# A twelve-layer decoder on one core: where the norms' inverse square roots are computed

## The reference, cut to what matters

```python
x = x + sublayer(_layernorm(x, axis=-1), ...)
# _layernorm: (x - mean) / sqrt(var + 1e-5)
```

## Time and profile before

| | |
|---|---|
| median of 3 runs | 1956.75 us (1954.98 to 1956.88) |
| the profiled execution, its own time | 1954.65 us |
| its span, first to last instruction | 1953.2 us |
| PE, DVE, ACT, POOL busy | 78%, 63%, 42%, 36% of the span |
| mean granted TensorE clock | 0.826 of full speed (2.4 GHz) |

### The profile page before, as it was taken

The page is one execution under the profiler, slowest core; times in us unless marked ns, Lnnn a source line. Parts: engine busy times, 40 slices in busy tenths (PEclk is TensorE's granted clock), DMA queues, the critical chain, the costliest instruction groups (busy, mean ns, idle before and its releaser), DMA issues. The chain is left out here.

```text
span 1953.2 us, 26886 instructions
## 1 busy us (share of the span) xinstructions
PE 1528.4 (78%) x8610; PEld 1058.0 (54%) x8610; DVE 1235.1 (63%) x3228; ACT 818.4 (42%) x2168; POOL 702.9 (36%) x975
## 2 busy tenths in 40 slices
PE   4899987799999589996953981154787689948998
PEld 3566754588888323334742550023555379944665
DVE  4587775365555688983347239896888679953222
ACT  1244431144333478883143113311777368811111
POOL 1488840066655457671001004343555222110000
PEclk8799995899999755556986995576899879958999
DMA  5100002000000155553000011101000300000000
GB/s 200 52 7 7 1 12 92 11 2 7 6 1 1 35 98 96 91 92 114 1 0 0 0 39 51 38 1 54 1 1 2 129 2 2 2 1 1 1 0 22
DMA packets 98379, 62.20 MB, mean 32 GB/s; under 512 B 88896, under 2 KB 93376, under 8 KB 96448
## 3 DMA queue, kind: packets, MB, share of 16 engines
q1 hardware_dynamic: 98240, 60.48, 11.6%
HBM read 38.44 MB, written 1.05 MB: 20 GB/s over the span
## 5 line engine op out<-in xcount | busy, mean ns | idle before, releaser
L101 PE MATMUL banks<-arena_a,normed_t 128*128 128x512 f32 (+3 forms) x736 | 281.9, 533 | 11.7 <-PEq L2963 11.7
L425 POOL TENSOR_TENSOR lut_weights<-lut_weights,arena_b 128x536 f32<-128x536 f32 x128 | 179.2, 1400 | 211.6 <-DVE arena_b L415 201.7
L101 PEld LDWEIGHTS banks<-arena_a,normed_t 128*128 128x128 f32 x736 | 140.6, 211 | 123.0 <-issue 120.0
L584 POOL TENSOR_SCALAR work<-work,small 128x256 f32<-128x256 f32 (+1 forms) x384 | 178.3, 482 | 76.5 <-DVE small L576 76.5
L101 PE MATMUL banks<-arena_a 64*128 64x512 bf16 (+1 forms) x384 | 161.7, 540 | 34.4 <-PEq L2963 18.6
L1506 ACT ACTIVATE arena_a<-banks,work 128x1024 uint8<-128x1024 f32 x128 | 154.1, 1204 | 48.3 <-DVE work L1450 40.5
L1448 DVE TENSOR_REDUCE work<-banks 128x1 f32<-128x1024 f32 x128 | 155.3, 1214 | 22.6 <-PE banks L101 22.6
L1535 POOL TENSOR_SCALAR arena_a<-arena_a 128x1024 bf16<-128x1024 uint8 x128 | 132.8, 1045 | 76.8 <-DMA arena_a<-arena_a 74.1
L564 ACT ACTIVATE work<-banks,small 128x256 f32<-128x256 f32 (+1 forms) x258 | 115.2, 458 | 63.3 <-DVE small L551 59.2
L107 PE MATMUL banks<-identity,work 128*128 128x128 f32 x968 | 133.1, 278 | 10.1 <-DVE work L1125 4.7
L107 PEld LDWEIGHTS banks<-identity,work 128*128 128x128 f32 x968 | 113.1, 146 | 24.7 <-issue 7.0
(11 more groups left out here) (420 smaller groups left out, 3510.0 us busy)
## 6 DMA issues: line engine op xcount, KB each, us to landing
arena_a<-in_L3f_wg SPq DMA_DIRECT2D x1, 4096.0 KB, 13.3
arena_b<-in_lut_idx SPq DMA_DIRECT2D x8, 268.0 KB, 2.9
arena_b<-in_L_wqn SPq DMA_DIRECT2D x1, 2048.0 KB, 12.4
arena_b<-in_L_wo SPq DMA_DIRECT2D x1, 2048.0 KB, 16.8
arena_a<-in_L_wq SPq DMA_DIRECT2D x1, 2048.0 KB, 7.5
arena_a<-in_L_wo SPq DMA_DIRECT2D x1, 2048.0 KB, 13.2
arena_a<-arena_a SPq DMA_TRANSPOSE x128, 2.5
arena_a<-in_L_wgu SPq DMA_DIRECT2D x1, 2048.0 KB, 9.8
```

The source lines that it names most:

```text
L101: ins = t.matmul(out, lhs_t, rhs, start=start and i == 0, stop=stop and i == n - 1)
L425: g.tensor_tensor(o, o, lut_t[j % 2], ALU.add).then_inc(*summed.up(c * LUT + j))
L584: ins = g.tensor_scalar(e[:, c], e[:, c], A.rl[n % 2][:, 2 * hh + i:2 * hh + i + 1], 0.0, ALU.mult, ALU.add)
```

## The change

GpSimd computes the inverse roots as `(value + eps) ** -0.5`: an add, and a power with a tile of exponents, -0.5 each, filled once at the start. At the twelve stage norms this pair is the first thing on GpSimd's list, right behind the barrier; VectorE waits for it before L330. At the other three VectorE hands its sum (`ssq`, `var`) to GpSimd and waits for the root. `r2`'s pair stands in front of the addition of L1891 on GpSimd's list.

```diff
-    def rsqrt(dst, src, tmp):
-        v.wait_ge(*vs.now())
-        v.tensor_scalar(dst.bitcast(I32), src.bitcast(I32), -0.5, float(0x5F3759DF), ALU.mult, ALU.add).then_inc(*vs.up())
-        for _ in range(3):
-            v.wait_ge(*vs.now())
-            v.scalar_tensor_tensor(tmp, dst, -0.5, dst, ALU.mult, ALU.mult).then_inc(*vs.up())
-            v.wait_ge(*vs.now())
-            v.tensor_tensor(tmp, tmp, src, ALU.mult).then_inc(*vs.up())
-            v.wait_ge(*vs.now())
-            v.scalar_tensor_tensor(dst, tmp, 1.5, dst, ALU.add, ALU.mult).then_inc(*vs.up())
+    def rsqrt_gpsimd(dst, src, more, s, name):
+
+        g.tensor_scalar(dst, src, 1.0, more, ALU.mult, ALU.add).then_inc(*gs.up())
+        g.wait_ge(*gs.now())
+        g.tensor_tensor(dst, dst, halves, ALU.pow).then_inc(*gs.up(s, name))
+
+    def norm_gpsimd(s):
+        rsqrt_gpsimd(rs, mv.rearrange("p (t k) -> p t k", k=2)[:, :, 1], LN_EPS, s, "rstd")
...
-        ve, nm = tiny[:, 0:8], tiny[:, 0:8]
-        v.tensor_scalar(ve, var[:, :, 1], LN_EPS, None, ALU.add).then_inc(*vs.up())
-        rsqrt(rs, ve, tiny[:, 8:16])
-        v.wait_ge(*vs.now())
+        nm = tiny[:, 0:8]
+        v.wait_ge(*(yield gs, s, "rstd"))
         v.scalar_tensor_tensor(nm, var[:, :, 0], -1.0, rs, ALU.mult, ALU.mult).then_inc(*vs.up(s, "scale"))
...
-            v.tensor_scalar(ssq, ssq, 1.0 / LORA, 1.1920928955078125e-07, ALU.mult, ALU.add).then_inc(*vs.up())
-            rsqrt(krs, ssq, tiny[:, 48:56])
-            v.wait_ge(*vs.now())
+            v.tensor_scalar(ssq, ssq, 1.0 / LORA, None, ALU.mult).then_inc(*vs.up(s, "ssq"))
+            v.wait_ge(*(yield gs, s, "krs"))
...
         def gpsimd():
+            norm_gpsimd(s)
             g.memset(W["tri"], 0.0).then_inc(*gs.up())
...
+            g.wait_ge(*(yield vs, s, "ssq"))
+            rsqrt_gpsimd(krs, ssq, 1.1920928955078125e-07, s, "krs")
...
-            v.tensor_scalar(var, var, 1e-6, None, ALU.add).then_inc(*vs.up())
-            rsqrt(r_, var, tiny[:, 48:56])
-            v.wait_ge(*vs.now())
+            v.wait_ge(*(yield gs, s, "r"))
...
         def gpsimd():
+            norm_gpsimd(s)
+            g.wait_ge(*(yield vs, s, "var"))
+            rsqrt_gpsimd(r_, var, 1e-6, s, "r")
...
+            g.wait_ge(*(yield vs, s, "ssq"))
+            rsqrt_gpsimd(r2, ssq, 1e-6, s, "r2")
             g.wait_ge(*(yield vs, s, "x1", NB - 1))
             g.tensor_tensor(x, x, nf, ALU.add).then_inc(*gs.up(s, "x"))
...
+        g.memset(halves, -0.5).then_inc(*gs.up())
```

More of the change, by code:

```diff
@@ L149, in build @@
     rs = sb("rstd", NT)
+    halves = sb("minus_half", NT)
     ctx_t = sb("context_t", KH * NB * S)
@@ L336, in norm_vector @@
     def norm_vector(s, nf, bank_of=None):
-        norm_scale(s)
+        yield from norm_scale(s)
         for b in range(NB):
@@ L1764, in vector @@
             v.wait_ge(*vs.now())
-            v.tensor_tensor(var, var, mv.rearrange("p (t k) -> p t k", k=2)[:, :, 1], ALU.mult).then_inc(*vs.up())
-            v.wait_ge(*vs.now())
-            v.tensor_scalar(var, var, 1e-6, None, ALU.add).then_inc(*vs.up())
-            rsqrt(r_, var, tiny[:, 48:56])
-            v.wait_ge(*vs.now())
+            v.tensor_tensor(var, var, mv.rearrange("p (t k) -> p t k", k=2)[:, :, 1], ALU.mult).then_inc(*vs.up(s, "var"))
+            v.wait_ge(*(yield gs, s, "r"))
             v.wait_ge(*normed_v.now())
@@ L1821, in vector @@
             v.wait_ge(*(yield as_, s, "squares"))
-            v.tensor_scalar(ssq, ssq, 1.0 / D, 1e-6, ALU.mult, ALU.add).then_inc(*vs.up())
-            rsqrt(r2, ssq, tiny[:, 72:80])
-            v.wait_ge(*vs.now())
+            v.tensor_scalar(ssq, ssq, 1.0 / D, None, ALU.mult).then_inc(*vs.up(s, "ssq"))
+            v.wait_ge(*(yield gs, s, "r2"))
             v.wait_ge(*(yield turned, s, "rec", NB - 1))
```

1 line of the change is left out of this document (added).

## The result

The changed kernel takes 1960.09 us (median of 12 runs, 1958.98 to 1962.51), the kernel before 1956.34 us in the same comparison (12 runs, 1954.5 to 1957.39). The ratio is 1.0021 with a 95% interval of 1.0012 to 1.003: slower by 0.21%, some 4 us, where 14.5 us of gain were forecast. The time lies inside the range, on the other side of the kernel before than forecast.

The account below looks back on a forecast made before the run. Bound by latency chains at inverse roots: eleven VectorE instructions, 2.22 us at a stage's start. Savings 5.7 + 0.7 + 1.2 + 0.8 + 3.0 + 2.1 + 0.85 + 0.1 = 14.5 us give 1942.3 us, range 1933 to 1968.

Parts of the forecast that it names:

- e = 0.5, the power at 0.7 us: In every pair on GpSimd, a power on 8 columns costs 0.5 us above an add, so 0.7 us.
- l0_ffn: 0: At l0_ffn's norm 0 us saved, as TensorE's first transposes start behind its own products.
- The rival with a code load (0.08): The power's code must be loaded, 5.6 us; once, chance 0.08; at every change of code, 0.02.
- Once: 1948: If the power's code is loaded only once, the kernel takes 1948 us, still faster; chance 0.08.
- r2: 3.0: In l2_attention, 4.0 us saved by freeing L1822 of GpSimd's addition, about 1.0 lost to slower L1714: 3.0 saved.
- l0_cross: 0.1: In l0_cross 0.1 us left of 0.95 gained, since the second reduction can't start before the pair is done.
- krs, r_, l2_attention's start, l2_cross, l3_attention: Savings there: krs 0.7, r_ 0.8, l2_attention's start 1.2, l2_cross and l3_attention 2.1 us together.
- l3_cross: 0.85: In l3_cross 0.85 us saved: pair hidden, ScalarE's L351 at most 1.25 earlier, VectorE's quantising perhaps held 0.4.
- The clock rival: With less idle TensorE at krs the clock might not fall during 20 us of folding: 1932 us; chance 0.06.
- Nothing comes through: Other engines end last at most places, so a gain under 3.9 us, about 1954; chance 0.07.
- The power is slow: GpSimd computes the power by a program and each stage waits; above 1.7 us longer than Newton; chance 0.22.
- two signs of being wrong: The power's row on GpSimd above 1.7 us, or the starts moving and the stages not.

Follow-up runs that it names:

- constant roots: The changed kernel with a product in place of the power and factors that make every inverse root constant: 1939.72 us, ratio 0.9915.
- both repairs: The changed kernel with a tiny GpSimd add right behind the second reduction, and l2_attention's addition waiting for VectorE's last L1718: 1949.35 us, ratio 0.997.

## Why the prediction was wrong

*e = 0.5, the power at 0.7 us.* This is the step that failed first. It was built by counting some thirty elementary steps at the price of an add, 2.2 ns a column, and the thirty come from no row. The runs show 1.65 us on 8 columns: 0.16 us for each column, which at 2.2 ns a step would be some seventy steps, and some 0.35 us besides, which the estimate left out. The break-even power was put at 1.7 us, and the measured one lies 0.05 below it: by the forecast's own sum the change comes to a gain of 14.5 - 14 x 0.95 = 1.2 us. The other parts of the pair were a little dear: 0.20 us, not 0.30, for the first instruction, 0.08 us, not 0.17, between the two, and less for the handovers. Together a place lost 0.70 us of what it was given, which is 0.95 - 0.25 at a clean start, and 9.8 us over fourteen: 4.7 us of gain would have been left. (Two small slips in the forecast's sums: by its rate e = 0 gives 14.5 + 7.0 = 21.5 us, not 20.5; and its fourteen places take in l3_cross, whose pair it calls hidden, so that its own places make thirteen.)

The bounds (0 to 2.8) did hold the price. The rule of the Trainium skill ("GPSIMD Engine Reference", "When to use GPSIMD") that elementwise work with two inputs costs about twice as much on GpSimd speaks of an add, a product or a maximum, and does not price a power. For a product the runs bear it out or better: 204 ns against the 166 of VectorE on 8 columns, and 1.26 us against the 0.69 of L1415 on 512. A power, 1657 ns, is ten times that same 166. The forecast took the rule for the whole pair, and so put the sum near its low end of time.

*l0_ffn: 0.* This is the step that turned the sign. The step looked at who needs the normalised tile, and not at what the first instruction on GpSimd must wait for. The forecast knew that the reduction's code must be loaded and timed it in l0_cross; that the ordinary code must then be loaded back it did not ask. The trace before had it twice: two configurations in front of L425, hidden by an idle GpSimd, and two in front of L860, whose row shows GpSimd idle for 27 us by "issue". The change made a critical instruction the first to need that code. Measured: 7.3 us lost, and 7.0 returned by one tiny addition. The rival with a code load (0.08) supposed that the power's own code is missing; the profile shows no configuration in front of a power except where a reduction went ahead, so that was not it. "Once: 1948" priced such a load at 5.6 us where 7.3 were lost, and gave it to the wrong owner. The Trainium skill ("GPSIMD Engine Reference", "Instruction dispatch") gives about 6 us for a first call of freshly loaded code; the 5.5 to 6.1 us in front of the reductions agree, where the reduction waited for nothing else, while the way back takes 6.8 to 8.0 us beside idle DMA engines and 10.1 to 10.9 at l0_ffn's start beside busy ones.

*r2: 3.0.* The first half is right (3.49 to 0.17 us). The second half, that the eight L1714 would each be "half as long again" beside the addition, is wrong in kind: one of them is held until the addition ends (4.70 us) and the others are not slowed at all. The 1045 ns of the earlier trace rows were most likely such a hold too, only of a shorter instruction: both slow ones start beside GpSimd's additions of L1522. Here is the second (timeline, then the first of the two L1522 by itself):

```profile
659.13 1.80 POOL L1522 TENSOR_TENSOR arena_a<-arena_a,big_b 128x256 f32<-128x256 f32 x2 [0.82 <-ACT big_b L1486]
659.35 1.04 DVE L1415 TENSOR_TENSOR arena_a<-arena_a 128x512 f32<-128x512 f32 x1
```

```profile
L1522 POOL TENSOR_TENSOR arena_a<-arena_a,big_b x1: 717/717/717, 659.1 to 659.1; 128x256 f32<-128x256 f32 x1
```

The first L1522 ends at 659.84, and L1415 0.55 us after it, where it needs 0.69 alone; the second L1522 takes 1.11 us in place of 0.67, as if it had waited for L1415 in its turn. "Half as long again" was thus no slowing that could be carried over to the eight L1714: what counts is how much of GpSimd's instruction is left.

The place around `r2` lost 0.9 us in place of gaining 3.0 - 0.7 = 2.3, so 3.2 us are missing. With the addition later the place gains 3.3 us, with or without power.

*l0_cross: 0.1.* The mechanism is right: the load for the reduction starts when the pair is done. The stage lost 1.05 us where 0.1 was to be gained; 0.7 of these 1.15 are the price of the pair, counted in the fourteen places, and 0.45 lie beyond.

*krs, r_, l2_attention's start, l2_cross, l3_attention.* With 0.70 less each these should give 0, 0.1, 0.5, 0.3 and 0.3. Measured: `krs` 2.23 us from L738 to L744 against 2.21; l2_attention's norm 0.59 earlier; l2_cross 0.36; l3_attention 0.27. All as the steps say, the size of the power aside. `r_`, from the product L1763 (L1767 after) to the first scaled block, takes 2.40 us in place of 2.61: 0.2.

*l3_cross: 0.85.* ScalarE's L348 is 1.36 us earlier after the statistics, as the step had it in kind: it now starts as ScalarE's L2761 ends, with no idle time ahead of it. The stage is 3.65 us shorter in this execution and 2.1 to 3.5 us in the others that compute it on GpSimd (191.91 to 193.23, against 195.38 and 195.32 before); the part above 1.4 is not explained.

*The sum.* 14.5 - 9.8 (price) - 3.2 (`r2`) - 7.3 (l0_ffn) - 0.45 (l0_cross) + 1.2 (l3_cross, with its 0.70 given back) = -5.05 us, and the spans differ by 5.5. The rest is within what unchanged stages vary. That the sum closes so well is in part luck: l2_ffn's -1.3 us and l3_attention's +1.1 of the table are in none of its terms and nearly cancel.

*The clock rival* could not come true here, since `krs` takes as long as before (the mean clock is 0.826 in both); with constant roots, where TensorE's idle time did shrink by 1.4 us, the clock fell all the same. *Nothing comes through* was wrong too: with constant roots the same chain is some 17 to 21 us shorter. *The power is slow* had the nearest mechanism, but at 1.65 us its price alone leaves a small gain; the loss needed the code load (without it 0.9988; without the held L1718 1.0006). Of its two signs of being wrong neither came: the power's row is just under 1.7 us, and the stages moved with the starts. No sign was named for what turned the result, a start that moves late.

The range held the time, but only by the rivals' share of it: the forecast's own 1935 to 1950, and its direction, failed.

## What to carry to other kernels

Before an elementwise function is moved to GpSimd, measure it by itself for the sizes that it will have: a product and a power are the same call in the program and cost 0.20 and 1.65 us on 8 columns, 1.26 and 82 us on 512. Look up which instruction of GpSimd is now the first behind each reduction over partitions, because the way back of the code lies in front of it; put a tiny instruction there where nobody waits. And when GpSimd's long instruction holds a short one of VectorE, move the long one to where nobody waits behind it: here that gained the same 3.3 us whether the root was computed by Newton's steps or by the power.

## What the hardware showed that was not expected

The power grows by 0.16 us for each column over the 128 partitions, where the product grows by about 2 ns a column. The code's way back takes 6.9 us (8.0 us in the kernel with both repairs) while the DMA engines stand idle, 10.2 us while they are busy for 91%. Beside the one addition of 4.5 us of GpSimd, one instruction of VectorE is held to its end (3.49 us for a product on 8 columns, 4.70 us for a scaled block) and the following ones run at full speed. Several short instructions of GpSimd in a row can hold one of VectorE as well: in the kernel before, the cast of the earlier trace rows waits through all six fills of L2604. In l3_attention the cast L2547, beside the same fills, took 1.93 us in the changed kernel and 0.41 us in the one with the late addition, and what decides between the two stays open.
